# Pair 0's x in six loads instead of four with two short last chunks, the exponentials' sum ahead of the diagonals, and fewer warm products

## The reference

```python
B, CIN, COUT, H, W, K, KH, KW = (32, 64, 64, 56, 56, 4, 3, 3)
g = _gn(x)                      # 32 groups of 2 channels, eps 1e-5
pooled = g.mean(axis=(2, 3))
a = relu(einsum('bc,kc->bk', pooled, fc1_w) + fc1_b)
att = softmax(einsum('bk,jk->bj', a, fc2_w) + fc2_b, axis=1)
agg_w = einsum('bk,koihw->boihw', att, weight)
agg_b = att @ bias
out = x + conv3x3_same(g, agg_w) + agg_b[:, :, None, None]
```

## Time and profile before

| | us |
|---|---|
| median of 3 runs | 305.23 |
| lowest and highest run | 304.73 and 305.49 |
| the profiled execution's own time | 304.7 |
| its span, from first to last instruction | 302.9 |
| TensorE busy in it | 297.3 |

### The profile page before, as it was taken

One profiled execution on the slowest core, in us unless ns is written; L12 is line 12 of the kernel. 1 busy time (PEld: TensorE's weight loads), 2 busy tenths in 40 slices (PEclk: granted clock), 3 DMA queues, 4 the chain that ended last, 5 costly groups with the idle time before them and its releaser, 6 DMA issues.

```text
span 302.9 us, 15877 instructions
## 1 busy us (share of the span) xinstructions
PE 297.3 (98%) x7066; PEld 273.2 (90%) x7066; DVE 246.0 (81%) x799; ACT 189.8 (63%) x246; POOL 17.7 (6%) x30
## 2 busy tenths in 40 slices
PE   8899999999999999999999999999999999999995
PEld 6678997799978997799999999999999999999874
DVE  3898998989999999998998989699696978956000
ACT  3766739194683927385496869567685866768222
POOL 2221040402100000000000000000000000000000
PEclk9999999999999999999999999999999999999999
DMA  7957875737547575846808898685758342332333
GB/s 266 307 166 191 284 231 161 218 131 197 161 150 224 161 208 173 225 157 170 239 26 236 243 232 276 155 257 164 209 135 235 96 122 70 111 101 80 95 112 104
DMA packets 26868, 53.62 MB, mean 177 GB/s; under 512 B 6064, under 2 KB 16432, under 8 KB 26800
## 3 DMA queue, kind: packets, MB, share of 16 engines
q1 hardware_dynamic: 26576, 52.53, 58.6%
q10 hardware_dynamic: 224, 0.07, 0.1%
HBM read 26.89 MB, written 25.69 MB: 174 GB/s over the span
## 4 chain that ended last, share of the span: by engine, by line
PE 95%; DMA 2%; DVE 1%; SPq 0%; issue 0%; POOL 0%; ACT 0%; DVEq 0%
PE acc L1063 94%; DMA x<-x 2%; SPq L315 0%; DVE stats L443 0%; PE tiny L1004 0%; PE acc L1031 0%; PE acc L1043 0%; POOL rstd L414 0%; DVE mv L478 0%; DVE o L791 0%; ACT wh L863 0%; PE tiny L1016 0%; DVE mix L642 0%; PE tiny L1010 0%; DVE sums L490 0%
## 5 line engine op out<-in xcount | busy, mean ns | idle before, releaser
L1063 PE MATMUL acc<-xh,wh 64*64 64x385 f16 (+5 forms) x2304 | 112.6, 325 | 0.3 <-ACT wh L863 0.3
L1063 PE MATMUL acc<-xh,wl 64*64 64x385 f16 (+5 forms) x2304 | 112.4, 325 | 0.0
L1063 PE MATMUL acc<-xl,wh 64*64 64x385 f16 (+5 forms) x2304 | 111.7, 325 | 0.0
L1063 PEld LDWEIGHTS acc<-xl,wh 64*64 64x64 f16 x2304 | 91.4, 107 | 5.9
L1063 PEld LDWEIGHTS acc<-xh,wl 64*64 64x64 f16 x2304 | 90.6, 107 | 6.7
L1063 PEld LDWEIGHTS acc<-xh,wh 64*64 64x64 f16 x2304 | 89.6, 107 | 7.4 <-ACT wh L863 0.5
L913 ACT ACTIVATE o<-acc,par 128x392 f32<-128x392 f32 (+1 forms) x64 | 43.0, 672 | 56.8 <-PE acc L1063 56.8
L457 DVE BATCH_NORM_STATS2 stats<-x 128x6 f32<-128x448 f32 x105 | 61.2, 618 | 1.9
L834 ACT ACTIVATE xh<-x,xof,xsc 128x1568 f16<-128x1568 f32 x24 | 40.5, 1692 | 25.2 <-DVE xof L544 24.7
L701 DVE TENSOR_TENSOR xl<-x,xh 128x1568 f16<-128x1568 f32 x28 | 49.8, 1783 | 3.4 <-ACT x L801 3.2
L592 DVE SCALAR_TENSOR_TENSOR mix<-w_sb,ex,mix 128x576 f32<-128x576 f32 (+1 forms) x69 | 42.9, 621 | 0.5
(11 more groups left out here) (106 smaller groups left out, 161.8 us busy)
## 6 DMA issues: line engine op xcount, KB each, us to landing
x<-x SPq DMA_DIRECT2D x60, 392.0 KB, 4.1
out<-o SPq DMA_DIRECT2D x36, 196.0 KB, 3.8
out<-o SPq DMA_DIRECT2D x72, 98.0 KB, 2.8
out<-o SPq DMA_DIRECT2D x8, 588.0 KB, 3.7
out<-o SPq DMA_DIRECT2D x16, 294.0 KB, 4.3
x<-x SPq DMA_DIRECT2D x3, 448.0 KB, 4.5
w_sb<-w_t SPq DMA_DIRECT2D x2, 576.0 KB, 3.9
out<-o SPq DMA_DIRECT2D x7, 112.0 KB, 2.2
```

Source lines behind the costliest of these rows:

```text
L1063: ins = nc.tensor.matmul(pixels[:, top:bottom, left:right], weights[i][halves[m], tap * C:(tap + 1) * C], window, start=start and step == ...
```

## The change

**Loads and statistics.** x of pair 0 comes in six transfers: two of two chunks, two of one chunk (448 pixels) and two of half a chunk (224). VectorE takes a statistic for each: chunks 0, 1, 3, 4 and 5, then two of 224 pixels. The values have a tile of their own, `first_stats`, with 48 columns instead of 42; the exchange and the aggregate of pair 0 run over it, and no longer over `stats`. `first_stats` was the name of the function; it is `statistics_of_first` now. The gate of the second half of w_sb and of the second group of warm products is again the last piece.

**Own means.** Since the short chunks weigh half, ScalarE takes the mean in two instructions: over the twelve values of the whole chunks after VectorE's statistic of chunk 5 (`s_most`), then over the four of the short ones, with the first result as bias, after the last statistic.

**Order.** In `first_mixture` the exponentials' sum stands in front of the two diagonals. In `first_range` the products of `std` come first and the product of `wnorms` last; the second product of `wnorms`, which only later pairs use, goes behind `part_sum` as `weights_range`, with a semaphore and a place in the other PSUM tile of its own.

**Warm products.** 38, 4, 6, 2, 3, 3 instead of 38, 8, 12, 6, 3, 3.

```diff
@@ -29,8 +29,9 @@
 CHUNK = 448
 CHUNKS = PIX // CHUNK
 
-PIECES = ((0, 2), (2, 4), (4, 5), (5, 7))
-PIECE_OF = (0, 0, 1, 1, 2, 3, 3)
+FIRST_CHUNKS = tuple((t * CHUNK, (t + 1) * CHUNK) for t in range(CHUNKS - 1)) + ((2688, 2912), (2912, PIX))
+PIECES = ((0, 896), (896, 1792), (1792, 2240), (2240, 2688), (2688, 2912), (2912, PIX))
+PIECE_OF = (0, 0, 1, 1, 2, 3, 4, 5)
 
 GATE = 0
 
@@ -55,7 +56,7 @@
 TURNED = (2, 3, 0, 1)
 
 X_RING = 4
-WARM_PRODUCTS = (38, 8, 12, 6, 3, 3)
+WARM_PRODUCTS = (38, 4, 6, 2, 3, 3)
 
 EARLY = 4
 
@@ -156,11 +157,13 @@
 
 
         stats = sb("stats", [P, 2, CHUNKS * 6])
+        first_stats = sb("first_stats", [P, 2, len(FIRST_CHUNKS) * 6])
+        own_part = sb("own_part", [P, 1])
         own = sb("own", [P, 2])
 
         moments = sb("moments", [P, 2])
         moment_square = sb("moment_square", [P, 1])
-        means = sb("means", [P, 2 * CHUNKS])
+        means = sb("means", [P, 2 * (CHUNKS + 1)])
         rtotal = sb("rtotal", [P, 1])
         mv = sb("mv", [P, 2])
         guess = sb("guess", [P, 1])
...
@@ -311,7 +316,7 @@
                     sp.dma_start(*lower_rows(p, m, g, groups)).then_inc(stored[i][1], 16)
 
             for n, (first, end) in enumerate(PIECES):
-                pixels = slice(first * CHUNK, end * CHUNK)
+                pixels = slice(first, end)
                 sp.dma_start(x_sb[0][:, pixels], x_d[0, :, pixels]).then_inc(x_piece[n], 16)
 
             for n, (piece, ks) in enumerate(((GATE, slice(0, 2)), (len(PIECES) - 1, slice(2, K)))):
@@ -359,7 +364,7 @@
 
         total = tiny[1][:, RANGE:RANGE + 1]
 
-        summed = stats[:, 0, 6 * SUMMED:6 * (SUMMED + 1)].rearrange("p (h v) -> p h v", v=3)
+        summed = first_stats[:, 0, 6 * SUMMED:6 * (SUMMED + 1)].rearrange("p (h v) -> p h v", v=3)
 
         @block.gpsimd
         def _(pool):
@@ -435,15 +440,18 @@
 
             swap = [n ^ 1 for n in range(32)]
 
-            def first_stats():
-
-                for t in range(CHUNKS):
+            def statistics_of_first():
+
+                for t, (first, end) in enumerate(FIRST_CHUNKS):
                     if t != SUMMED:
                         dve.wait_ge(x_piece[PIECE_OF[t]], 16)
-                        ins = nc.vector.bn_stats(stats[:, 0, 6 * t:6 * t + 6], x_sb[0][:, t * CHUNK:(t + 1) * CHUNK])
+                        ins = nc.vector.bn_stats(first_stats[:, 0, 6 * t:6 * t + 6], x_sb[0][:, first:end])
+                        if t == CHUNKS - 2:
+                            ins.then_inc(s_most, 1)
                 ins.then_inc(s_stats, 1)
                 dve.wait_ge(s_summed, 2)
-                exchange_stats(0)
+                dve.wait_ge(s_stats, 1)
+                nc.vector.stream_shuffle(first_stats[:, 1, :], first_stats[:, 0, :], swap).then_inc(s_other, 1)
 
             def chunk_stats(p, start=0, end=CHUNKS):
                 for t in range(start, end):
@@ -467,17 +475,16 @@
 
             def exchange_stats(p):
                 dve.wait_ge(s_stats, p + 1)
-                if p >= 1:
-                    dve.wait_ge(s_eps, p)
+                dve.wait_ge(s_eps, p)
                 nc.vector.stream_shuffle(stats[:, 1, :], stats[:, 0, :], swap).then_inc(s_other, 1)
 
             def first_group_stats():
 
                 tt, ts, stt = nc.vector.tensor_tensor, nc.vector.tensor_scalar, nc.vector.scalar_tensor_tensor
                 dve.wait_ge(s_other, 1)
-                nc.vector.bn_aggr(mv[:], stats[:].rearrange("p a b -> p (a b)")).then_inc(s_mv, 1)
+                nc.vector.bn_aggr(mv[:], first_stats[:].rearrange("p a b -> p (a b)")).then_inc(s_mv, 1)
                 dve.wait_ge(s_mv, 1)
-                dve.wait_ge(s_own, 1)
+                dve.wait_ge(s_own, 2)
                 tt(diff[:], own[:, 0:1], mv[:, 0:1], ALU.subtract).then_inc(gch, 1)
                 ts(gm[0][:], mv[:, 0:1], 1.0, None, ALU.mult)
                 dve.wait_ge(s_const, 4)
@@ -575,7 +582,7 @@
                 if k == 0:
                     dve.wait_ge(s_exsum, 1)
                     nc.vector.reciprocal(rsum[:], exsum[:]).then_inc(dch, 1)
-                    dve.wait_ge(s_range, 3)
+                    dve.wait_ge(s_range, 1)
                     nc.vector.reciprocal(rtotal[:], total).then_inc(dch, 1)
                 elif k == 1:
                     dve.wait_ge(dch, 4)
@@ -626,10 +633,10 @@
                 dve.wait_ge(s_exp, 1)
                 part = PARTS[0]
                 dve.wait_ge(s_const, 3)
+                nc.vector.tensor_reduce(exsum[:], ex[:], AX.X, ALU.add).then_inc(s_exsum, 1)
 
                 for k in range(SUMMED_SHARES):
                     nc.vector.tensor_scalar(diagonals[:, k, :], eye[:], ex[:, k:k + 1], None, ALU.mult).then_inc(s_diagonal, 1)
-                nc.vector.tensor_reduce(exsum[:], ex[:], AX.X, ALU.add).then_inc(s_exsum, 1)
                 dve.wait_ge(s_weights[1], 16)
                 nc.vector.tensor_scalar(part_mix[:], w_sb[:, 2, part], ex[:, 2:3], None, ALU.mult).then_inc(s_part, 1)
                 first_scale_step(0)
@@ -680,8 +687,8 @@
 
             def weights_bound():
 
-                dve.wait_ge(s_range, 3)
-                nc.vector.tensor_scalar(wbound[:], tiny[1][:, WEIGHTS:WEIGHTS + 1], 1.0 / C, None,
+                dve.wait_ge(s_weights_range, 1)
+                nc.vector.tensor_scalar(wbound[:], tiny[0][:, WEIGHTS:WEIGHTS + 1], 1.0 / C, None,
                                         ALU.mult).then_inc(s_bound, 1)
 
             def low_weights(p):
...
@@ -885,10 +892,17 @@
 
             def own_means():
 
+                channel = first_stats[:, 0, :].rearrange("p (n v) -> p n v", v=3)
+                whole, halved = channel[:, 0:2 * (CHUNKS - 1), 1], channel[:, 2 * (CHUNKS - 1):, 1]
                 act.wait_ge(s_summed, 1)
+                act.wait_ge(s_most, 1)
+
+                nc.scalar.activation(means[:, 0:2 * (CHUNKS - 1)], whole, ACT.Identity, scale=0.125 / CHUNKS,
+                                     accum_out=own_part[:]).then_inc(s_own, 1)
                 act.wait_ge(s_stats, 1)
-                nc.scalar.activation(means[:], stats[:, 0, :].rearrange("p (n v) -> p n v", v=3)[:, :, 1], ACT.Identity,
-                                     scale=0.5 / CHUNKS, accum_out=own[:, 0:1]).then_inc(s_own, 1)
+                act.wait_ge(s_own, 1)
+                nc.scalar.activation(means[:, 2 * (CHUNKS - 1):2 * (CHUNKS + 1)], halved, ACT.Identity, bias=own_part[:],
+                                     scale=0.25 / CHUNKS, accum_out=own[:, 0:1]).then_inc(s_own, 1)
 
             def exponentials(p):
                 act.wait_ge(s_logit, p + 1)
@@ -1012,14 +1026,18 @@
 
             def first_range():
 
-                pe.wait_ge(s_wnorms, 1)
-                nc.tensor.matmul(tiny[1][:, WEIGHTS:WEIGHTS + 1], scale[:], wnorms[:],
-                                 start=True, stop=True).then_inc(s_range, 1)
-                nc.tensor.matmul(tiny[1][:, RANGE:RANGE + 1], scale[:], wnorms[:], start=True, stop=False)
+
                 pe.wait_ge(s_first_std, 1)
                 for m in range(2):
                     nc.tensor.matmul(tiny[1][halves[m], RANGE:RANGE + 1], ones[halves[m], 0:C], std[0][halves[m], :],
-                                     start=False, stop=True).then_inc(s_range, 1)
+                                     start=True, stop=False)
+                pe.wait_ge(s_wnorms, 1)
+                nc.tensor.matmul(tiny[1][:, RANGE:RANGE + 1], scale[:], wnorms[:], start=False, stop=True).then_inc(s_range, 1)
+
+            def weights_range():
+
+                nc.tensor.matmul(tiny[0][:, WEIGHTS:WEIGHTS + 1], scale[:], wnorms[:],
+                                 start=True, stop=True).then_inc(s_weights_range, 1)
 
             def part_sum():
 
@@ -1096,6 +1114,7 @@
             first_range()
             keep_warm(3)
             part_sum()
+            weights_range()
             keep_warm(4)
 
             pe.wait_ge(s_part, 2)
```

4 lines of the change are left out of this document (3 added, 1 removed).

## The result

The changed kernel took 306.18 us in the median of 20 runs (304.39 to 307.83), the kernel before 305.03 us in 20 runs (304.73 to 306.00). The ratio is 1.0031, with a 95% interval of 1.0016 to 1.0045: slower by 0.3%. (The ratios in this text are those of the means.) My forecast was 304.8 us with a range to 305.7 us; it was wrong, and in the direction of the rival to which I gave 0.12.

A forecast was written before the change was run, and what follows sets the result against it. TensorE, busy 98% of the span, was taken as the bound, so an earlier first main product ends the kernel earlier. -0.42 + 0.06 - 0.11 = -0.47 us gave a median of 304.8 us, range 304.1 to 305.7 us.

The forecast's parts named there:

- the rival to which I gave 0.12: TensorE's clock falls because warm products are removed: 305.7 or 306.3 us by where the fall lies; chance 0.12.
- so no product waited for them to end: The ten warm products removed ahead of the sums stood before 0.41 us of TensorE idling, so removing them delays nothing.
- a fall that begins at 11.7 us: Clock rival: 2.1 us of low clock ahead of the first main product, 1.05 us behind it; 305.7 us.
- one inside the main products: Clock rival: a 3.15 us stretch of low clock in the main products loses half of it; 306.3 us.
- The last statistics, -0.42 us: VectorE's last statistics, on smaller pieces that land earlier, end at 8.05 us instead of 8.47 us.
- small packets: Loads of 224 columns have 896-byte packets: last piece lands at up to 7.67 us, w_sb 0.1 to 0.3 us later.
- The aggregate, +0.06 us: Pair 0's aggregate goes from 84 to 96 values, costing 0.06 us on top of 0.53 us.
- The sum ahead of the diagonals and fewer warm products there, -0.11 us: part_sum's first product waits for the diagonal, not for warm products: 12.11 us instead of 12.22 us, others unchanged.
- What is hidden: Work beside the chain (ScalarE and GpSimd's chunk, the wnorms product, w_sb's landing) was claimed to stay covered.
- Cover for both: wnorms' total (11.1 to 11.3 us) and w_sb's second half (11.0 to 11.4 us) precede VectorE's need; 0.4 us cover at worst.
- the third term: The -0.11 us for part_sum's earlier start, from the sum ahead of the diagonals and four fewer warm products.

The follow-up runs named there:

- b1: The kernel before with only the new warm product counts (38, 4, 6, 2, 3, 3): 306.17 us, ratio 1.0041 to before.
- d2: a3 with six of the twelve warm products behind the last statistic taken out (38, 8, 6, 6, 3, 3): 304.93 us, ratio 1.0003 to before.
- d1: a3 with four warm products behind the last landing taken out (38, 4, 12, 6, 3, 3): 304.53 us, ratio 0.9989 to before.
- d3: The changed kernel with the old warm counts and the old four loads, still with eight statistics: 305.07 us, ratio 0.9995 to before.
- a1: The changed kernel with the old warm product counts (38, 8, 12, 6, 3, 3), six loads: 304.97 us, ratio 0.9993 to before.
- a2: a1 with the exponentials' sum again behind the two diagonals: 305.00 us, ratio 0.9997 to before.
- c2: a3 with four warm products ahead of part_sum taken out (38, 8, 12, 2, 3, 3): 304.61 us, ratio 0.9981 to before.
- a3: a1 with the last 448 columns in one load (five loads), still two short statistics: 304.53 us, ratio 0.9989 to before.
- c3: a3 with eight warm products taken out of the first group (30, 8, 12, 6, 3, 3): 304.55 us, ratio 0.9982 to before.
- d4: a3 with eight fewer warm products at the start and four more behind the last statistic (30, 8, 16, 6, 3, 3): 304.61 us, ratio 0.9990 to before.

## Why the prediction was wrong

**The forecast's step that failed** is the one about warm products: "so no product waited for them to end". That was true and beside the point. I counted them as work in the way of other work and as nothing once they were out of the way; what they held was the clock, which I had as a rival at 0.12. It happened in 14 of 20 runs. I argued against the rival with the idle stretches being 1.3 us at most, and with the small products between them. The idle stretches were 0.9 us at most, and the clock fell all the same. Neither argument had a row behind it, since before never showed TensorE so little used behind its rise. I had also misread the row that I had: I wrote that six of the twelve warm products lay between 8.7 and 11.7 us before, but the earlier trace rows has all twelve between 8.53 and 10.00 us, so TensorE did more there than I counted. The page that I named, "TensorE: Matmul & The Clock Gate" of the Trainium skill, says in Part 1 that activity releases the throttle, and b1 agrees: with less of it, 11 of 12 runs had a fall. With that rule and no row against it, the chance should have been near a half, and the range should have reached 307 us.

**The price of a fall** came out near, but not by my working. I gave 305.7 us for a fall that begins at 11.7 us and 306.3 us for one inside the main products; the runs at 0.991 to 0.994 have a median of 306.18 us, 1.7 us over the held ones. Ahead of the main products I had stretched only part_sum, by 0.4 us. It grew by 0.67 us in b1, and the warm products behind it, which I hadn't counted, grew by about 0.6 us in the traces of the change and of b1 and hold up the first main product. So the cheap case isn't cheap: d2, with the fall wholly ahead of the main products, took 306.60 us in the profiled execution, d1 304.98 us. The runs at 0.987 or 0.988 come to 307.36 us, 2.9 us over the held ones. I hadn't reckoned with such runs, and no trace of one was taken; whether they have a longer stretch or a second one stays open.

**The last statistics, -0.42 us.** Right in mechanism and nearly in size: 0.39 us forecast for a short statistic, 0.38 us measured; its end 8.05 us forecast, 8.11 us measured, so -0.36 us. d3 shows that this gain is the landing's: without a load of 448 columns that lands before the last one, nothing is left of it. The second split of the load, for which I had weighed small packets at length, isn't needed for it, and a1 and a2 hint that it costs something.

**The aggregate, +0.06 us.** Right: 0.59 us for 0.53 us.

**The sum ahead of the diagonals and fewer warm products there, -0.11 us.** Not confirmed. a2 shows 0.03 us for the sum's place, and c2, with part_sum at its diagonal, is no faster than a3. c2's profile names one reason, a late second half of w_sb; no trace of c2 with that half early was taken.

**What is hidden.** "Cover for both" was wrong in this execution. I had put the first half of w_sb 0.1 to 0.3 us late; it was 0.8 us late, and I had followed it only through wnorms to the total; the second half, for which I took 3.7 us, took 4.8 us and used up its cover. One place where it hurt is ScalarE's queue: the first inputs and the exponentials stand behind the squares, and VectorE waited for them. The other is the wnorms product, behind which part_sum stood. It had been covered in the rows of before, where the landing was at its early value, and I took one execution's landing for a property of the kernel.

**The held runs.** 304.49 us against 304.76 us worked out, with -0.54 us for -0.47 us. The sum of terms was close, in part by luck: the third term isn't shown, only six runs held, and from lowest to lowest run the gain is 0.34 us. a3's trace, in which w_sb landed early, has its first main product 0.31 us earlier than before.

## What to carry to other kernels

Before taking out work that only keeps TensorE busy, ask what clock the engine will have afterwards, and treat that as the first question, not as a rival at the end: at most half a microsecond of shorter head was paid for with 1.7 us in the runs with the shorter loss of clock, and warm products that were left stood in the way themselves once they ran at half clock. Look at the mean granted clock of every run, not only at the profiled one; a median over two or three groups hides both the gain and the loss. And of a late-landing transfer follow every instruction queued behind the one that waits for it, on its own engine first.

A version that keeps the old warm counts and the two short statistics, with five loads (a3), was faster than before by a tenth of a per cent: 304.53 us, ratio 0.9989 (0.9981 to 0.9998), against 1.0031 for the change as it was made. c2, c3, d1 and d4 (304.53 to 304.61 us) aren't told apart from it.
